# Mixture-of-experts output: slots sorted by expert, and gathers begun during the last blocks

## The reference

```
w, sel = _route(x, gate_weight, expert_bias)     # 4 of 16 experts for each token, 4 weights
for each expert e (g, u, d of shape 256x512, 256x512, 512x256):
    y   = silu(x @ g.T) * (x @ u.T) @ d.T
    acc = acc + w_e[:, None] * y                 # w_e is zero for tokens that did not choose e
out = x2 + acc + silu(x @ sg.T) * (x @ su.T) @ sd.T
```

## Time and profile before

| | |
|---|---|
| median of 3 runs (lowest to highest) | 1540.34 us (1539.63 to 1545.67) |
| the profiled execution: time | 1537.91 us |
| the profiled execution: span from first to last instruction | 1536.1 us |
| busy: PE, DVE, ACT, POOL | 1358.9, 800.6, 735.7, 575.1 us |
| mixture of experts, from the first block's inputs to the end | about 1239 to 1536.1 us |

### The profile page before, as it was taken

The page is one execution under the profiler, slowest core; times in us unless marked ns, Lnnn a source line. Parts: engine busy times, 40 slices in busy tenths (PEclk is TensorE's granted clock), DMA queues, the critical chain, the costliest instruction groups (busy, mean ns, idle before and its releaser), DMA issues. The chain is left out here.

```text
span 1536.1 us, 22738 instructions
## 1 busy us (share of the span) xinstructions
PE 1358.9 (88%) x7136; PEld 1104.9 (72%) x7136; DVE 800.6 (52%) x1362; ACT 735.7 (48%) x1741; POOL 575.1 (37%) x346
## 2 busy tenths in 40 slices
PE   5997799999999999999966999997799989999950
PEld 4775577777777777777744888886677767887740
DVE  4433465757575656565624444443499832333225
ACT  2443465656565655555524677777411223333320
POOL 2122232333333333333013333332356494259826
PEclk9999799999999999999987999998899999999985
DMA  5796540504141313232415111113643266456537
GB/s 201 236 288 176 214 163 1 201 19 177 41 167 51 139 79 128 91 123 96 178 43 183 45 63 56 48 48 103 235 151 110 90 233 213 151 179 246 179 99 216
DMA packets 78984, 209.79 MB, mean 137 GB/s; under 512 B 5888, under 2 KB 39168, under 8 KB 72960
## 3 DMA queue, kind: packets, MB, share of 16 engines
q1 hardware_dynamic: 69472, 163.78, 30.1%
q0 software_dynamic: 7136, 38.80, 7.4%
q10 hardware_dynamic: 2304, 6.29, 1.1%
HBM read 154.59 MB, written 92.01 MB: 161 GB/s over the span
## 5 line engine op out<-in xcount | busy, mean ns | idle before, releaser
L660 DVE TENSOR_TENSOR probsT_lo<-psTr,probsT_hi 128x512 fp32r<-128x512 f32 x256 | 176.4, 690 | 200.5 <-ACT probsT_hi L610 200.2
L610 ACT CAST probsT_hi<-psTr 128x512 fp32r<-128x512 f32 x256 | 150.0, 586 | 211.7 <-PE psTr L750 210.9
L750 PE MATMUL psTr<-ident,probs 128*128 128x128 f32 x1024 | 152.6, 276 | 18.9 <-DVE probsT_lo L660 12.9
L750 PEld LDWEIGHTS psTr<-ident,probs 128*128 128x128 f32 x1024 | 122.2, 141 | 62.3 <-DVE probsT_lo L660 29.1
L527 POOL TENSOR_TENSOR ctxT_lo<-ctx_f,ctxT_hi 128x512 fp32r<-128x512 f32 x32 | 41.3, 1292 | 321.1 <-ACT ctxT_hi L579 321.1
L655 DVE TENSOR_REDUCE nmax<-psS 128x1 f32<-128x1024 f32 x128 | 155.4, 1214 | 11.5 <-PE psS L66 10.7
L572 ACT ACTIVATE probs<-psS,nmax 128x1024 f32<-128x1024 f32 x128 | 143.5, 1121 | 28.5 <-DVE nmax L655 28.5
L64 PE MATMUL bank<-w_slots,ao_first_hi 128*128 (+1 forms) x252 | 107.0, 425 | 16.1 <-DVE w_slots L1731 9.3
L64 PE MATMUL psV<-probsT_hi,kv_hi 128*128 128x512 f32 x256 | 117.3, 458 | 2.0
L64 PE MATMUL psS<-kT_hi,qe 128*128 128x512 f32 x256 | 112.9, 441 | 5.6 <-issue 4.7
L1461 POOL TENSOR_TENSOR w_slots<-w_ahead,w_slots 128x3072 fp32r<-128x3072 f32 x15 | 102.2, 6811 | 1.2
(11 more groups left out here) (258 smaller groups left out, 3321.4 us busy)
## 6 DMA issues: line engine op xcount, KB each, us to landing
w_ahead<-w_exp POOLq DMA_DIRECT2D x14, 1536.0 KB, 7.3
qe<-stage SPq DMA_DIRECT2D x16, 1024.0 KB, 6.7
qe<-qe SPq DMA_DIRECT2D x16, 1024.0 KB, 5.1
wraw<-w_pairs SPq DMA_DIRECT2D x8, 1792.0 KB, 11.3
early<-xs SPq DMA_DIRECT2D x47, 256.0 KB, 3.0
xs<-h_rows SPq DMA_DIRECT2D x47, 256.0 KB, 2.0
early<-ctx SPq DMA_DIRECT2D x16, 512.0 KB, 3.5
ao<-attn_out SPq DMA_DIRECT2D x32, 256.0 KB, 2.4
```

Source lines behind the costliest of these rows:

```text
L610: act.copy(PT[k % PTN].hi[:], psT[slot][:]).then_inc(turned_hi, 1)
L660: dve.tensor_tensor(out, psT[slot][:], f32(hi), ALU.subtract).then_inc(turned_free, 1)
L750: last = pe.transpose(psT[slot][:, q * P:(q + 1) * P], src(q), ident[:])
```

## The change

Each token's four slots are sorted in ascending order, and with them the weights, so that choice k = 0 is the lowest expert. The sort (`sort_slots`) is nine DVE instructions for all eight token tiles at once, 128x128 or 128x32 elements; one stands behind `gated(i)` in each of the blocks i = 8 to 16. The gathers are ordered by choice (k outer, token tile inner), each into a place of its own: 12 in `w_ahead` and 20 in the two places of `w_slots` that held the experts 12 and 13. Before the eight gathers of choice k, POOL waits until the blocks of all experts up to 12 + k have landed in `xs`; SP counts landed blocks (`y_landed`), which adds a wait for block i-1 ahead of the write of block i. For k < 3 a gather also waits until the one three before it has landed (`ON_WAY`), and every gather for the one five before it. DVE adds the first 16 gathers four at a time, behind `gated` of the blocks 44, 45 and 46 and at the very end of the loop, and the other 16 after it. A token tile goes out after its addition of choice 3. The scratch `pair_sums` moves into `cmp_experts` to make room.

```diff
-XR, YR, GR, HR = 4, 3, 12, 3
+XR, YR, HR = 4, 3, 3
+SORT_AT = 8
+ON_WAY = 3
...
+    dead = [(NE - 4) % NSLOT * SLOT, (NE - 3) % NSLOT * SLOT]
+    G = [ahead[:, j * BANK:(j + 1) * BANK] for j in range(2 * wcol // BANK)]
+    G += [f32(WS[:, at + j * BANK:at + (j + 1) * BANK]) for at in dead for j in range(2 * wcol // BANK)]
...
+        def landed(i):
+            sp.wait_ge(y_out[i % YR], 16 * (i // YR + 1))
+            sp.sem_inc(y_landed, 1)
...
         for i in range(NTILE):
+            if i >= 1:
+                landed(i - 1)
             sp.wait_ge(y_made, i + 1)
...
+        landed(NTILE - 1)
         for tt in range(NT):
-            sp.wait_ge(comb, TOPK * (tt + 1))
+            sp.wait_ge(comb, NT * (TOPK - 1) + tt + 1)
...
-        for j in range(YR):
-            pool.wait_ge(y_out[j], 16 * len(range(j, NTILE, YR)))
         pool.wait_ge(w_ready, NE)
+        pool.wait_ge(sorted_made, 1)
         for g in range(NT * TOPK):
-            tt, k = g // TOPK, g % TOPK
-            wait(pool, comb, g - GR + 1)
-            pool.indirect_dma_start(G[g % GR], None, rows,
-                                    bass.IndirectOffsetOnAxis(ap=pos_i[:, tt, k:k + 1], axis=0)).then_inc(
-                                        g_in[g % GR], 16)
+            k, tt = g // NT, g % NT
+            if tt == 0:
+                e = NE - TOPK + k
+                pool.wait_ge(y_landed, pool.value_load(cum_i[0:1, e:e + 1], min_val=1, max_val=NTILE + 1))
+                pool.sem_inc(gather_free, 1)
+            if k < TOPK - 1 and g >= ON_WAY:
+                pool.wait_ge(g_in[(g - ON_WAY) % 5], 16 * ((g - ON_WAY) // 5 + 1))
+            wait(pool, g_in[g % 5], 16 * (g // 5))
+            pool.indirect_dma_start(G[g], None, rows,
+                                    bass.IndirectOffsetOnAxis(ap=pos_si[:, tt, k:k + 1], axis=0)).then_inc(
+                                        g_in[g % 5], 16)
...
+        def sort_slots(step):
+            big = [P, NT, TOPK, TOPK]
+            src, dst = ((pos_all, pos_s), (cw, cw_s))[step > 5]
+            if step == 0:
+                link(dve.tensor_tensor(cmp_k, pos_all[:].unsqueeze(2).to_broadcast(big),
+                                       pos_all[:].unsqueeze(3).to_broadcast(big), ALU.is_lt))
+            elif step == 1:
+                link(dve.tensor_reduce(rank_k[:], cmp_k, AX.X, ALU.add))
+            elif step in (2, 6):
+                link(dve.tensor_tensor(cmp_k, rank_k[:].unsqueeze(2).to_broadcast(big),
+                                       c_row(C_K, TOPK).unsqueeze(1).unsqueeze(3).to_broadcast(big), ALU.is_equal))
+            elif step in (3, 7):
+                link(dve.tensor_tensor(cmp_k, cmp_k, src[:].unsqueeze(2).to_broadcast(big), ALU.mult))
+            elif step in (4, 8):
+                link(dve.tensor_reduce(dst[:], cmp_k, AX.X, ALU.add))
+            else:
+                dve.tensor_copy(pos_si[:], pos_s[:]).then_inc(sorted_made, 1)
...
+        def combine(g):
+            k, tt = g // NT, g % NT
+            dve.wait_ge(g_in[g % 5], 16 * (g // 5 + 1))
+            wait(dve, comb, g - NT + 1)
+            dve.scalar_tensor_tensor(acc[:, tt, :], G[g], cw_s[:, tt, k:k + 1], acc[:, tt, :], ALU.mult,
+                                     ALU.add).then_inc(comb, 1)
...
             if i < NTILE:
                 gated(i)
-        for g in range(NT * TOPK):
...
+            if SORT_AT <= i < SORT_AT + 9:
+                sort_slots(i - SORT_AT)
+            if i >= NTILE - 3:
+                for g in range((i - NTILE + 3) * NT // 2, (i - NTILE + 4) * NT // 2):
+                    combine(g)
+        for g in range(2 * NT, NT * TOPK):
+            combine(g)
```

More of the change, by code:

```diff
@@ L1313, in build_moe @@
     sig, V = sb("scores", [P, NT, NE]), sb("biased", [P, NE])
[L1314 removed]
+    gsum = sb("group_sum", [P, NG])
     cmp_g, grank, pen = sb("cmp_groups", [P, NG, 2, NG]), sb("group_rank", [P, NG]), sb("penalty", [P, NG])
@@ L1320, in build_moe @@
     kx, wk, wsum = sb("choice_x", [P, TOPK, NE]), sb("choice_w", [P, TOPK]), sb("choice_sum", [P, 1])
-    pos_f, pos_k = sb("slot_of", [P, NE]), sb("slot_k", [P, TOPK])
+    pos_f = sb("slot_of", [P, NE])
     pos_i = sb("slot_int", [P, NT, TOPK], mybir.dt.int32)
@@ L1324, in build_moe @@
     full, cum, tabx = sb("tiles_of", [P, NE]), sb("tiles_to", [P, NE]), sb("table_cols", [P, 4])
+    pairs = cmp_e[:].rearrange("p i a j -> p (i a j)")[:, 0:NG * GS * GS].rearrange(
+        "p (g i j) -> p g i j", i=GS, j=GS)
+    cmp_k = cmp_e[:].rearrange("p i a j -> p (i a j)")[:, 0:NT * TOPK * TOPK].rearrange(
+        "p (t i j) -> p t i j", i=TOPK, j=TOPK)
+    rank_k, pos_s, cw_s = (sb(n, [P, NT, TOPK]) for n in ("slot_rank", "slot_sorted", "weight_sorted"))
+    pos_all = sb("slot_all", [P, NT, TOPK])
+    pos_si = sb("slot_sorted_int", [P, NT, TOPK], mybir.dt.int32)
     full_c, spare = cmp_e[:].rearrange("p i a j -> p (i a j)")[:, 0:NE * NT].rearrange(
@@ L1358, in build_moe @@
     Y = [HN[:, j, :] for j in range(YR)]
-    G = [ahead[:, j * BANK:(j + 1) * BANK] for j in range(GR)]
+    dead = [(NE - 4) % NSLOT * SLOT, (NE - 3) % NSLOT * SLOT]
+    G = [ahead[:, j * BANK:(j + 1) * BANK] for j in range(2 * wcol // BANK)]
+    G += [f32(WS[:, at + j * BANK:at + (j + 1) * BANK]) for at in dead for j in range(2 * wcol // BANK)]
     rows = t["xs"].rearrange("b p c -> (b p) c")
@@ L1382, in build_moe @@
     tile_done, y_made, y_out = sem("tile_done"), sem("y_made"), [sem(f"y_out{j}") for j in range(YR)]
-    g_in, comb, out_sem = [sem(f"g_in{j}") for j in range(GR)], sem("comb"), sem("out_done")
+    y_landed, sorted_made, gather_free = sem("y_landed"), sem("sorted_made"), sem("gather_free")
+    g_in, comb, out_sem = [sem(f"g_in{j}") for j in range(5)], sem("comb"), sem("out_done")
     M = 2 * NIT
@@ L1648, in route_groups @@
             vg = V[:].rearrange("p (g x) -> p g x", x=GS)
-            link(dve.tensor_tensor(pairs[:], vg.unsqueeze(2).to_broadcast([P, NG, GS, GS]),
+            link(dve.tensor_tensor(pairs, vg.unsqueeze(2).to_broadcast([P, NG, GS, GS]),
                                    vg.unsqueeze(3).to_broadcast([P, NG, GS, GS]), ALU.add))
-            link(dve.tensor_tensor(pairs[:], pairs[:], diag.unsqueeze(1).to_broadcast([P, NG, GS, GS]), ALU.add))
-            link(dve.tensor_reduce(gsum[:], pairs[:].rearrange("p g i j -> p g (i j)"), AX.X, ALU.max))
+            link(dve.tensor_tensor(pairs, pairs, diag.unsqueeze(1).to_broadcast([P, NG, GS, GS]), ALU.add))
+            link(dve.tensor_reduce(gsum[:], pairs.rearrange("p g i j -> p g (i j)"), AX.X, ALU.max))
             gj = gsum[:].unsqueeze(1).to_broadcast([P, NG, NG])
@@ L1687, in slots @@
             link(dve.tensor_tensor(kx[:], K[tt % 2][:], pos_f[:].unsqueeze(1).to_broadcast([P, TOPK, NE]), ALU.mult))
-            link(dve.tensor_reduce(pos_k[:], kx[:], AX.X, ALU.add))
-            dve.tensor_copy(pos_i[:, tt, :], pos_k[:]).then_inc(pos_made, 1)
+            link(dve.tensor_reduce(pos_all[:, tt, :], kx[:], AX.X, ALU.add))
+            dve.tensor_copy(pos_i[:, tt, :], pos_all[:, tt, :]).then_inc(pos_made, 1)
         def table_cols():
@@ L1726, in _ @@
         dve.sem_inc(tile_done, 1)
+        dve.sem_inc(y_landed, 1)
         free(dve.memset(seen[0][:], 0.0))
```

6 lines of the change are left out of this document (removed).

## The result

The changed kernel takes **1517.99 us** in the median of 4 runs (1517.16 to 1521.14), beside 1541.01 us (1539.63 to 1545.67) for the kernel before: a ratio of 0.9849, 95% interval 0.9823 to 0.9875. That is 23.0 us less, where 24.5 were predicted. The profiled execution took 1518.74 us with a span of 1516.9, against the earlier trace rows; so the two profiles lie 19.2 us apart, and what the medians have on top is spread between executions, to which the experiments come back.

A forecast was written before the change was run, and what follows sets the result against it. The program ends with POOL's gathers, which wait for PE's last block. 1536.1 - 30.9 + 2.5 + 0.7 + 3.2 = 1511.6 us, 24.5 less; taken off the median, 1515.8 us. Own range 1512 to 1520, with rivals 1509 to 1522.

The forecast's parts named there:

- First gather: Start of POOL's last stage: at 1454.4, after its last weight subtraction, 30.9 us ahead of the earlier 1485.31.
- The sort's step 6: DVE behind block 14: two SBUF inputs, held by POOL's subtraction for expert 6 until about 1322.9, stalling PE 2.45 us.
- half of a clock penalty: PE after the stall in block 14: the clock may fall, taken as 0.8 us, with 0 and 1.6 as ends.
- the term of 3.2: Whole cost of the sort in the blocks: PE's stall of 2.45 us plus 0.8 for the clock.
- Rival (a): The sort hides entirely, with no hold by POOL's subtraction: 3.2 us less, 1512.6 us; 17%.
- Rival (b): The sort's step 1, a reduction with one SBUF input, is held too: 2.4 to 4.0 us more, 1518.2 to 1519.8; 10%.
- The 24 steps: Gathers 0 to 23, three on their way: landings set 1.47 us a step, 33.8 us for 23 steps (29.0 to 39.8).
- Gathers 24 to 31 and the end: Last eight gathers: 11.5 us with a read; then 8.0 us to the program's end plus 0.7 for outputs.
- Rival (c): Three on their way don't limit; gathers go by POOL's own 1.26 us a step: 4.8 us saved, 1511.0 us; 12%.
- (d): Gathers land late beside the blocks, making the kernel slower than before, from a landing of 7.3 us; 3%.
- (e): A gate opens only after the last block, so the prices are paid without the gain: 1546.7 us; 2%.
- The additions in the blocks cost nothing: DVE in blocks 44 to 46: 3.2 us of additions each time delay only dummy blocks, at no cost.

The follow-up runs named there:

- sort_at_10: The changed kernel with the sort begun at block 10 instead of 8: 1515.42 us, ratio 0.9858 to the kernel before.
- sort_at_12: The changed kernel with the sort begun at block 12 instead of 8: 1519.73 us, ratio 0.9885 to the kernel before.
- on_way_2: The changed kernel with two gathers allowed on their way instead of three: 1532.22 us, ratio 0.9936 to the kernel before.
- gate_last: The changed kernel with gathers waiting for all 47 blocks and all additions behind the loop: 1545.69 us, ratio 1.0030 to the kernel before.
- on_way_4: The changed kernel with four gathers allowed on their way instead of three: 1537.23 us, ratio 0.9970 to the kernel before.
- on_way_5: The changed kernel with five gathers allowed on their way instead of three: 1532.18 us, ratio 0.9960 to the kernel before.
- after_hidden: The changed kernel with POOL's weight copy for expert 1 waiting for DVE's last hidden_low: 1520.29 us, ratio 0.9892 to the kernel before.

## Why the prediction held, point by point

The prediction was right in its mechanism and within 2.2 us in its time, and a part of that closeness is luck. Its profiled sum was 1511.6 against a span of 1516.9; the 5.3 us are 2.9 of a step that it lacks, and 2.4 of terms sized too low. In the median 3.2 of these 5.3 don't show, because the profiled execution of the kernel before lay 2.4 us below its median and that of the changed kernel 0.8 above.

One of its own signs of being wrong appeared: the stretch up to the first gather was to grow by no more than 5 us, and POOL's last subtraction ends 6.8 us later than before (1460.49 against 1453.69). 2.9 of these stand at the result copy of block 8 already, ahead of the sort (1295.75 against 1292.82); the other 3.9 are the sort's stretch.

- **First gather.** Right: `w_ready` and not a gate on blocks decides, and POOL's subtraction is the last thing ahead. The start behind it was sized 0.76 us and measured 1.44.
- **The sort's step 6.** Right, as sort_at_10 and sort_at_12 show too: held where it meets the subtraction, 0.28 us where it doesn't, 5.46 where 5.6 was expected. PE's wait was 2.05 us, and block 14 took 7.13 instead of 4.82 by its result copies. The half of a clock penalty, 0.8 us, did not come in this execution, where the granted clock stayed at 1.00; in four of the nine profiles with this stall it came, with some 0.9 us. Blocks 15 and 17 took 0.5 and 0.4 more than before, so the term of 3.2 measured 3.8 from the copy of block 8 to that of block 26, and 4.0 from block 13 to 27; what these small waits are I did not settle. Rival (a), no hold, did not occur: the step in this place took 5.3 to 5.7 us in all nine.
- **Rival (b), the reduction held as well.** Wrong: 0.28 us inside the subtraction. The rule of the Trainium skill that the prediction set beside it (page "SBUF — State Buffer", section "Who interferes with whom") is borne out on both sides. But the page excepts VectorE's modes with two ports, copies among them, which the prediction leaves out, and the copy of 0.71 us in sort_at_10, held with one SBUF input, agrees with the exception.
- **The 24 steps.** Predicted 33.8 us, measured 34.86, that is 1.52 a step and not 1.47. on_way_2 shows the formula itself.
- **Gathers 24 to 31 and the end.** Predicted 11.5 and 8.7, measured 11.48 and 8.63.
- **Rival (c), POOL's own pace.** Its condition was made true by the runs with 4 and 5, and the conclusion was false: the blocks stop, and the time is 1532 to 1537 us instead of 1511.0. The prediction looked at the gathers' cost to themselves, and of the blocks' cost only at DMA landings.
- **Rivals (d) and (e).** (d) did not occur: landings have a median of 4.1 and a largest of 6.2 beside the blocks, where it takes 7.3. gate_last is (e) made real, with the additions behind the loop, at 1545.69 us where 1546.7 was worked out. That they agree is in part luck: the first gather came 5.3 us later than (e) has it, and the gathers took 1.9 less.
- **The additions in the blocks cost nothing.** Right as far as the runs tell, and the reason incomplete: four took 2.73 us, not 3.2. That they may also keep DVE from holding POOL later was not seen.
- **What was missed.** The hold of `hidden_low`. The prediction searched the sort's steps for meetings with POOL and took everything ahead of block 8 as unchanged. The work there is; the timing between two engines, a microsecond from a hold of 3.4 us, isn't the same from execution to execution. The delay of 2.9 us that was left of it at block 8 is in the pair of profiles and was not shown to be in the change.

## What to carry to other kernels

When a last stage waits for everything though its parts need only some, reorder the data so that each part has a gate of its own, and price the new start by what then comes last, here POOL's weights. Leave gaps in a stream of indirect transfers beside work on other engines: the 32 gathers took 3.5 us longer with three on their way, and with four or five most of the gain is lost. Place every DVE instruction with two SBUF inputs, the short ones too, and copies from SBUF to SBUF away from POOL's long ones, remember that long DVE work with two SBUF inputs holds POOL's indirect issues in turn, and look for such meetings in the parts that the change does not touch: single executions differ by some microseconds there.

## What the runs showed of the hardware

- ACT stood idle up to 13.62 us while gathers followed each other every 1.26 us, with no releaser in the profile, in on_way_4 and on_way_5; in one execution of after_hidden it stood idle up to 10.64 us at 1.36 us a gather. With the same 24 gathers at 1.5 us it did not. The cause is open.
- Holding goes both ways. A 128x128 comparison was held by POOL's subtraction, 5.46 us instead of 0.28. POOL's indirect issue beside DVE's 128x3072 subtraction took 2.96 or 4.45 us instead of about 1 and ended 0.85 after it, in all 14 profiles; beside unbroken additions one took 7.15 us in one trace.
- A copy of 128x32 elements with one SBUF input took 0.66 to 0.73 us instead of 0.17 where it met the end of POOL's subtraction, in three profiles. A reduction of 128x128 elements in the middle of one took 0.28.
- PE stalls of 1.89 to 2.26 us in the same place left the granted clock at 1.00 (the 2.4 GHz level) in five profiles, and in four it was 0.50 to 0.67 in the 2 us behind (0.50 is the 1.2 GHz level). After a stall of 3.46 us the stretch behind it had 0.57.
